# Adding two coefficient tables on GpSimd before the token products of the last three chunks of a one-core vision tower

## The chip, the cores and the metric

The kernel runs on one core of one Trainium2 chip. The metric is the device time of one execution, in microseconds (us), as the median of several executions. Engines are named PE (TensorE), DVE (VectorE), ACT (ScalarE), POOL (GpSimd) and SP (the queue that issues most DMAs).

## The reference, cut to what matters

The input `x` has shape (16, 256, 64, 2): 16 images, 256 channels h, 64 complex coefficients n. A first layer turns it into tokens; attention, an MLP and a tree of gates follow. Only the first layer is touched:

```python
dtA = A * dt[:, None]
dA = (1.0 + dtA / 2) / (1.0 - dtA / 2)
C_term = C * B[None]                                  # C is x, as complex numbers
V = jnp.exp(jnp.log(dA)[:, :, None] * jnp.arange(L))  # powers 0 to 255 of dA
K = 2.0 * jnp.einsum('chn,hnl->chl', C_term, V).real  # (16 images, 256 channels, 256 positions)
```

## The kernel before, in words

All data are float32. The exponent l of a power is split in three: a shift d (ND = 4 of them), an a (NA = 8) and an e (NE = 8), so that 4 x 8 x 8 = 256. For a channel, the result is a product over 128 rows, which are the real and the imaginary parts of the 64 coefficients: `Wa` and `Wb` (tiles of [128, 2, CH, B, ND], two buffers, by the chunk's parity) hold the image's coefficients turned by the 4 shifts, 16 images x 4 shifts = 64 columns for a channel, and `M` ([128, 2, CH, NA, NE]) holds the 64 powers of (a, e). `Wa` takes the coefficients times the real part of the shift, `Wb` the crosswise coefficients times the imaginary part; both are multiplied by the same `M` and added in PSUM. Column d = 0 of `Wb` is set to zero once, at the start; column d = 0 of `Wa` is the coefficients themselves.

The 256 channels go in 16 chunks of CH = 16. For a chunk n:

- SP loads its coefficients `craw` (`load_c`, L364), which waits for POOL's count `wdone` of the chunk two before it.
- POOL makes `Wa` and `Wb` for d = 1 to 3 (`rotate`, L510, the operation is at L522, 128x768), and waits for the token products two chunks before (`tokmm`), whose buffer it reuses.
- ACT fills d = 0 of `Wa` and e = 0 of `M` (`operands`, L702), and copies the X and Y tables to PSUM (`tables`, L709).
- DVE makes two products (`single_product`, L1178, the operation is at L1150, 128x896), into PSUM (`Ma[0]`) and into SBUF (`Mb`), and adds them into `M` for e = 1 to 7 (`single_sums`, L1185, L1190).
- PE makes the token products (`tokens`, L1641, the matmuls at L1652): 16 channels x 2 products; even channels write PSUM rows 0 to 63, odd ones rows 64 to 127. The profile shows two matmul instructions for each product. Then ACT copies the bank to `tokev` (`token_row`, L715, L719), and SP stores it (`store_h0`, L383).

Chunk 10 (`SINGLE`) is made in another way, in `unsummed_products` (DVE, L1170) and `unsummed_tokens` (PE, L1656): DVE writes its two products to `M` and `Mc` and doesn't add them, and PE makes four products per channel, `Wa` and `Wb` each with `M` (64 columns) and with `Mc` (56 columns, into the places e = 1 to 7, L1672).

From chunk FIRST = 12 on, the chunks are interleaved with the first steps of the next stage: step s = n - 12 goes with chunk n. A step takes two images of a half of the channels through norm 1, q, k and v:

- DVE: `norm1_stats(s + 3)` (L1223, L1226), then POOL: `scales` (L525: L530, L531, L533), then DVE: `norm1_apply` (`xh`, L1234), two steps ahead of its use.
- PE: `y_transposes(s + 1)` (L1688, needs `xh` of that step), `q_products(s)` (L1692), `kv_products(s, 0)` and `(s, 1)` (L1703, whose matmuls stand at L343 to L345), then the tokens of chunk n, in this order.
- ACT: `token_row(n - 1)`, `y_high(s + 1)` (L756, L761 and L764), `q_parts(s)`, `operands(n + 1)`, `tables(n + 1)`, `kv_parts` (L774).
- DVE: the products and the sum of chunk n, `y_low(s + 1)` (L1251), `q_elu(s)` (L1260), `norm1_apply(s + 2)`, `norm1_stats(s + 3)`, `k_elu` (L1271).
- POOL, for n = 12, 13, 14: `rotate` of chunk n + 1, then `scales(n - 9)`; then `scales(6)` and the later ones.

The order on each engine is the order in which the program writes it, and every wait is written by hand. Steps 4 and later have no chunk. Steps run to 15, and from then on a loop over groups of 512 tokens does the attention, the MLP and the tree.

Of the kernel before, what the change touches and what calls it, by code (L numbers as in the profile page):

```python
# [5 lines left out]
ALU = mybir.AluOpType  # L6
# [13 lines left out]
NE = 8  # L20
NA = 8
ND = 4
SH = NA * NE
CH = 16
# [16 lines left out]
STEPS = 2 * GROUPS  # L41
FIRST = 12
SINGLE = 10
SPREAD = STEPS - 5
STATS = {4: (7,), 5: (8,), 6: (9,), 7: (10, 11), 8: (12,), 9: (13,), 10: (14,), 11: (15,)}
LEVELS = 8
# [16 lines left out]
def vit_tower(nc, logdt, inv_ar, a_im, b_ri, c_ri, n1g, n1b, qkvT, projT, proj_b, n2g, n2b, fc1T, fc1_b,  # L63
              fc2T, fc2_b, wq, routersT, leafT, woutT, wout_b, consts, out):
    with ExitStack() as ctx:
# [248 lines left out]

        def added(n):

            return n + 1 - (n >= SINGLE)

        def sums_before(c):
            return max([x for x in range(c) if sums_bank(x) == sums_bank(c)], default=-1)  # L320
# [28 lines left out]
        def _(sp):  # L349
# [14 lines left out]
            def load_c(it, par):  # L364

                n = 2 * it + par
                sp.wait_ge(c0done, CREDIT + n - 1)
                sp.wait_ge(wdone, CREDIT + 2 * n - 3)
                sp.dma_start(craw[:, par, 0, :, :], c_ri[:, :, bass.ds(n * CH, CH), :].rearrange(
                    "r n h c -> (r n) h c")).then_inc(cld[par], 16)  # L370
                sp.wait_ge(wdone, CREDIT + 2 * (n - 1))
                for r in range(2):
                    sp.dma_start(craw[r * N:(r + 1) * N, par, 1, :, :],
                                 c_ri[1 - r, :, bass.ds(n * CH, CH), :]).then_inc(crossld[par], 16)
# [102 lines left out]
        def _(pool):  # L477
# [32 lines left out]
            def rotate(it, par):  # L510
# [3 lines left out]
                for x, w in enumerate((Wa, Wb)):  # L514
                    if x == 0:
                        pool.wait_ge(cld[par], CREDIT + 16 * (it + 1))
                    else:
# [4 lines left out]
                    pool.tensor_tensor(w[:, par, :, :, 1:ND].rearrange("p h c d -> p d h c"), c, u,  # L522
                                       ALU.mult).then_inc(wdone, 1)

            def scales(s):  # L525

                pool.wait_ge(st1, CREDIT + 4 * (s + 1))
                v = mv1[:, s, :, 1]
                pst = pst1[:, s, :, :]
                pool.tensor_scalar(pst[:, 0, :], v, EPS, None, ALU.add).then_inc(r1done, 1)  # L530
                pool.tensor_scalar(pst[:, 1, :], v, 1.0 + EPS, EPS * EPS, ALU.mult, ALU.add).then_inc(r1done, 1)  # L531
                pool.wait_ge(r1done, CREDIT + 3 * s + 2)
                pool.tensor_tensor(mr[:, 1:3, s // GROUPS, image(s, 0):image(s, 0) + 2], pst[:, 0:2, :],  # L533
                                   halfpow[:, :, 0:2], ALU.pow).then_inc(r1done, 1)
# [15 lines left out]
            scales(2)  # L550
            pool.wait_ge(xh1, CREDIT + 2 * 2 + 2)
            for n in range(FIRST, CHUNKS - 1):
                rotate((n + 1) // 2, (n + 1) % 2)
                scales(n - FIRST + 3)
            scales(CHUNKS - FIRST + 2)
            pool.wait_ge(b1copied, 1)
# [498 lines left out]
        def _(dve):  # L1055
# [114 lines left out]
            def unsummed_products(n):  # L1170
# [4 lines left out]
                product(n, 7, 0, M[:, n % 2, :, :, 1:NE])  # L1175
                product(n, 7, 1, Mc[:, :, :, :])

            def single_product(n, r):  # L1178

                if r == 0:  # L1180
                    dve.wait_ge(xyld, CREDIT + n + 1)
                    dve.wait_ge(vdone, CREDIT + added(n - 1))
                product(n, 7, r, (Ma[0], Mb[:, :, :, :])[r])
# [109 lines left out]
            norm1_stats(2)  # L1293
            for n in range(FIRST, CHUNKS):
                s = n - FIRST
                if s > 0:
                    single_product(n, 0)
                    single_product(n, 1)
                single_sums(n)
                if s == 0:  # L1300
                    norm1_apply(1)
                    norm1_apply(2)
                if s > 0:
                    y_low(s + 1)
                q_elu(s)
                if s > 0:
                    norm1_apply(s + 2)
                else:
                    k_elu(s, 0)
                    y_low(s + 1)  # L1310
                norm1_stats(s + 3)
                if s > 0:
                    k_elu(s, 0)
                k_elu(s, 1)
# [325 lines left out]
        def _(pe):  # L1640
            def tokens(n, par, b):  # L1641
# [11 lines left out]
                                       M[:, par, i, :, :].rearrange("p a e -> p (a e)"), start=x == 0, stop=x == 1)  # L1653
                mm.then_inc(tokmm, 1)

            def unsummed_tokens(n):  # L1656

                pe.wait_ge(wdone, CREDIT + 2 * (n + 1))
# [109 lines left out]
            for n in range(FIRST, CHUNKS):  # L1768
# [6 lines left out]
                    y_transposes(s + 1)  # L1775
                kv_products(s, 1)
                pe.wait_ge(tokout, CREDIT + n)
                tokens(n, n % 2, None)

            def step(s):  # L1780
                if s + 1 < STEPS:
# [309 lines left out]
```

## Time and profile before

| | |
|---|---|
| median of 3 runs | 489.0 us (487.67 to 489.45) |
| the profiled execution | 489.43 us, its span 487.6 us |
| PE busy | 439.4 us (90% of the span) |
| DVE, ACT, POOL busy | 346.5, 295.8, 192.2 us |
| token products at L1652 | 960 matmul instructions, 39.7 to 107.8 us |
| chunks 12 to 15 with steps 0 to 3 | about 80 to 108 us |

The span runs from the first to the last instruction; the execution's own time is 1.8 us longer. Chunks 13, 14 and 15 are the PE stretches at L1652 that begin at 92.2, 99.0 and 105.9 us. Busy time of PE is modelled at its end: consecutive matmuls overlap, so the distance between starts is what one costs.

### The profile page before, as it was taken

How to read it: one execution, taken by the hardware profiler on the slowest of the kernel's cores; microseconds unless marked ns; L12 is line 12 of the kernel's file. 1: busy time of each engine (PE TensorE's matmuls, PEld its weight loads, DVE VectorE, ACT ScalarE, POOL GpSimd, SP SyncE). 2: the span in 40 equal slices, each digit the busy share in tenths (PEclk: the TensorE clock that was granted, in tenths of full speed). 3: DMA queues.
4: the chain of work that ended last, by engine and by line, in shares of the span. 5: the costliest groups of instructions: out<-in, count | busy, mean ns of one | idle time of the engine just before them, and what ended most of it. 6: DMA issues, size and time to landing. Idle time of an engine off the chain costs nothing.

```text
span 487.6 us, 11439 instructions
## 1 busy us (share of the span) xinstructions
PE 439.4 (90%) x3881; PEld 401.9 (82%) x3881; DVE 346.5 (71%) x814; ACT 295.8 (61%) x620; POOL 192.2 (39%) x188
## 2 busy tenths in 40 slices
PE   1367778999999999999999999999999999998994
PEld 0157667887798898988998998998998998998994
DVE  5999987887876785537576576576586486484685
ACT  5754655979867686457357357357366367366552
POOL 0796997832423010516306306306306406405221
PEclk9877999999999999999999999999999999999998
DMA  4543777436343102001002002002002001001002
GB/s 130 175 149 82 177 191 219 115 88 171 98 135 102 37 33 64 3 1 44 1 2 86 0 0 86 0 0 86 0 0 86 0 0 43 0 0 44 2 1 86
DMA packets 39903, 30.95 MB, mean 63 GB/s; under 512 B 19520, under 2 KB 35264, under 8 KB 39872
## 3 DMA queue, kind: packets, MB, share of 16 engines
q1 hardware_dynamic: 28864, 27.41, 18.8%
q10 hardware_dynamic: 11008, 3.15, 2.8%
q8 instruction: 16, 0.26, 0.2%
q14 instruction: 15, 0.12, 0.1%
HBM read 17.97 MB, written 12.58 MB: 63 GB/s over the span
## 4 chain that ended last, share of the span: by engine, by line
PE 70%; DVE 9%; POOL 7%; issue 6%; ACT 4%; DMA 2%; DVEq 0%; POOLq 0%; SPq 0%; ACTq 0%
PE PS L343 20%; PE PS L345 19%; PE PS L344 19%; PE PS L1679 5%; PE PS L1721 3%; POOL Wb L522 3%; PE PS L1652 2%; DVE bst L1381 2%; PE PS L1688 1%; PE PS L1806 1%; POOL Wa L522 1%; DVE gl L1404 1%; DMA h<-h_scratch 1%; DMA iar<-in_inv_ar 1%; DVE outb L1435 1%
## 5 line engine op out<-in xcount | busy, mean ns | idle before, releaser
L877 ACT ACTIVATE PS<-PS,fc1bias 128x512 f32<-128x512 f32 x56 | 36.8, 656 | 76.5 <-PE PS L345 76.4
L343 PE MATMUL PS<-fc2h,gh 128*128 128x256 f32 x256 | 74.8, 292 | 3.7 <-DVE gl L1404 2.3
L575 POOL TENSOR_SCALAR pst<-mv 128x4 f32<-128x4 f32 x15 | 4.3, 283 | 180.0 <-DVE pst L1388 180.0
L345 PE MATMUL PS<-fc2l,gh 128*128 128x256 f32 x256 | 71.4, 279 | 0.0
L344 PE MATMUL PS<-fc2h,gl 128*128 128x256 f32 x256 | 71.3, 279 | 0.0
L1404 DVE TENSOR_TENSOR gl<-PS,gh 128x512 fp32r<-128x512 f32 x56 | 38.6, 690 | 37.9 <-ACT gh L880 35.2
L343 PEld LDWEIGHTS PS<-fc2h,gh 128*128 128x128 f32 x256 | 48.0, 188 | 9.0 <-DVE gl L1404 3.0
L343 PE MATMUL PS<-x2Th,fc1h 128*128 (+2 forms) x144 | 54.5, 378 | 0.0
L344 PE MATMUL PS<-x2Th,fc1l 128*128 (+2 forms) x144 | 53.0, 368 | 0.0
L345 PE MATMUL PS<-x2Tl,fc1h 128*128 (+2 forms) x144 | 52.9, 367 | 0.0
L344 PEld LDWEIGHTS PS<-fc2h,gl 128*128 128x128 f32 x256 | 48.2, 188 | 0.8
L345 PEld LDWEIGHTS PS<-fc2l,gh 128*128 128x128 f32 x256 | 48.0, 188 | 0.0
L1652 PE MATMUL PS<-M,Wa 128*64 128x64 f32 x480 | 32.1, 234 | 8.3 <-ACT Wa L727 3.5
L1652 PEld LDWEIGHTS PS<-M,Wa 128*64 128x64 f32 x480 | 29.8, 144 | 11.0 <-issue 6.1
L880 ACT ACTIVATE gh<-PS 128x512 fp32r<-128x512 f32 x56 | 33.6, 599 | 2.8
L1652 PE MATMUL PS<-M,Wb 128*64 128x64 f32 x480 | 31.5, 230 | 0.0
L345 PEld LDWEIGHTS PS<-x2Tl,fc1h 128*128 128x128 f32 x144 | 27.1, 188 | 4.7
L1652 PEld LDWEIGHTS PS<-M,Wb 128*64 128x64 f32 x480 | 29.8, 146 | 0.0
L343 PEld LDWEIGHTS PS<-x2Th,fc1h 128*128 128x128 f32 x144 | 27.1, 188 | 2.5
L344 PEld LDWEIGHTS PS<-x2Th,fc1l 128*128 128x128 f32 x144 | 27.2, 189 | 2.3
L522 POOL TENSOR_TENSOR Wa<-craw,U 128x768 f32<-128x768 f32 x16 | 26.4, 1652 | 6.5 <-PE PS L1652 4.2
L522 POOL TENSOR_TENSOR Wb<-craw,U 128x768 f32<-128x768 f32 x16 | 26.5, 1656 | 0.0
(259 smaller groups left out, 1407.4 us busy)
## 6 DMA issues: line engine op xcount, KB each, us to landing
h<-h_scratch SPq DMA_DIRECT2D x16, 256.0 KB, 3.4
q_scratch<-qe SPq DMA_DIRECT2D x16, 256.0 KB, 2.3
qf<-q_scratch SPq DMA_DIRECT2D x16, 256.0 KB, 3.0
out_tokens<-outb SPq DMA_DIRECT2D x14, 256.0 KB, 2.3
h_scratch<-tokev ACTq DMA_DIRECT2D x10, 256.0 KB, 3.2
craw<-in_c_ri SPq DMA_DIRECT2D x16, 128.0 KB, 2.6
craw<-in_c_ri SPq DMA_DIRECT2D x32, 64.0 KB, 2.4
h_scratch<-tokev SPq DMA_DIRECT2D x6, 256.0 KB, 2.9
```

The costliest lines, as they stand in the source:

```text
L343: pe.matmul(dst, ah, bh, start=start, stop=False, **kw)
L344: pe.matmul(dst, al, bh, start=False, stop=False, **kw)
L345: return pe.matmul(dst, ah, bl, start=False, stop=stop, **kw)
L522: pool.tensor_tensor(w[:, par, :, :, 1:ND].rearrange("p h c d -> p d h c"), c, u, ALU.mult).then_inc(wdone, 1)
L877: act.activation(bank(j % 2), bank(j % 2), ACT.Gelu, bias=fc1bias[:, j:j + 1]).then_inc(gact, 1)
L880: act.activation(gh[:, j % 2, :], bank(j % 2), ACT.Copy).then_inc(gact, 1)
L1381: dve.bn_stats(bst[:, t, :], x[:, t, :]).then_inc(done, 1)
L1404: dve.tensor_tensor(gl[:, j % 2, :], bank(j % 2), gh[:, j % 2, :].bitcast(F32), ALU.subtract).then_inc(gldone, 1)
L1435: dve.tensor_tensor(outb[:, 2 * b:2 * b + 2, :], PS[:, 6 + b, :].rearrange("p (t d) -> p t d", t=2), o1[:, 2 * b:2 * b + 2, :], ALU.add).t ...
L1652: mm = pe.matmul(dst, w[:, par, i, :, :].rearrange("p c d -> p (c d)"), M[:, par, i, :, :].rearrange("p a e -> p (a e)"), start=x == 0, st ...
L1679: mm = pe.transpose(PS[:, b + k, t * P:(t + 1) * P], src[:, t, k * P:(k + 1) * P], ident)
L1721: mm = pe.matmul(PS[:, sums_bank(c), k * (P + 1):(k + 1) * (P + 1)], key, value, start=half == 0 and k == 0, stop=half == 1, skip_group_ch ...
```

## The change

For chunks 13 to 15, POOL adds `Wb` onto `Wa` (d = 1 to 3) after it has made both, so that PE needs one product per channel in place of two. For chunk 15, DVE no longer adds its two products: it writes the first one to `M` and the second one to `Mb`, and PE makes a product with each. The count `wdone` now grows by three for these chunks, and the waits on it are rewritten to the same events as before (`made`). Chunk 12 and the earlier ones are as before.

```diff
+APART = 15
         def added(n):
-            return n + 1 - (n >= SINGLE)
+            return n + 1 - (n >= SINGLE) - (n >= APART)
+        def made(n):
+            return 2 * (n + 1) + max(0, n - FIRST)
...
             def load_c(it, par):
-                sp.wait_ge(wdone, CREDIT + 2 * n - 3)
+                sp.wait_ge(wdone, CREDIT + made(n - 3) + 1)
...
-                sp.wait_ge(wdone, CREDIT + 2 * (n - 1))
+                sp.wait_ge(wdone, CREDIT + made(n - 3) + 2)
...
+            def summed(n):
+                rotate(n // 2, n % 2)
+                pool.wait_ge(wdone, CREDIT + made(n - 1) + 2)
+                a, b = (w[:, n % 2, :, :, 1:ND].rearrange("p h c d -> p d h c") for w in (Wa, Wb))
+                pool.tensor_tensor(a, a, b, ALU.add).then_inc(wdone, 1)
...
             for n in range(FIRST, CHUNKS - 1):
-                rotate((n + 1) // 2, (n + 1) % 2)
+                summed(n + 1)
                 scales(n - FIRST + 3)
...
+            def apart_products(n):
+                dve.wait_ge(xyld, CREDIT + n + 1)
+                dve.wait_ge(tokmm, CREDIT + n - 1)
+                dve.wait_ge(vdone, CREDIT + added(n - 1))
+                product(n, 7, 0, M[:, n % 2, :, :, 1:NE])
+                product(n, 7, 1, Mb[:, :, :, :])
...
-                if s > 0:
+                if s > 0 and n != APART:
                     single_product(n, 0)
                     single_product(n, 1)
-                single_sums(n)
+                if n == APART:
+                    apart_products(n)
+                else:
+                    single_sums(n)
...
+            def summed_tokens(n):
+                pe.wait_ge(wdone, CREDIT + made(n))
+                pe.wait_ge(c0done, CREDIT + n + 1)
+                pe.wait_ge(m0done, CREDIT + n + 1)
+                pe.wait_ge(vdone, CREDIT + added(n))
+                for i in range(CH):
+                    rows = slice(64 * (i % 2), 64 * (i % 2) + 64)
+                    mm = pe.matmul(PS[rows, 0, (i // 2) * SH:(i // 2 + 1) * SH],
+                                   Wa[:, n % 2, i, :, :].rearrange("p c d -> p (c d)"),
+                                   M[:, n % 2, i, :, :].rearrange("p a e -> p (a e)"), start=True, stop=True)
+                mm.then_inc(tokmm, 1)
+            def apart_tokens(n):
...
+                pe.wait_ge(prodX, CREDIT + n + 1)
+                pe.wait_ge(prodY, CREDIT + n + 1)
+                for i in range(CH):
+                    rows = slice(64 * (i % 2), 64 * (i % 2) + 64)
+                    dst = PS[rows, 0, (i // 2) * SH:(i // 2 + 1) * SH]
+                    c = Wa[:, n % 2, i, :, :].rearrange("p c d -> p (c d)")
+                    pe.matmul(dst, c, M[:, n % 2, i, :, :].rearrange("p a e -> p (a e)"), start=True, stop=False,
+                              skip_group_check=True)
+                    mm = pe.matmul(dst.rearrange("p (a e) -> p a e", a=NA)[:, :, 1:NE], c, Mb[:, i, :, :], start=False,
+                                   stop=True, skip_group_check=True)
+                mm.then_inc(tokmm, 1)
...
                 pe.wait_ge(tokout, CREDIT + n)
-                tokens(n, n % 2, None)
+                if n == FIRST:
+                    tokens(n, n % 2, None)
+                elif n == APART:
+                    apart_tokens(n)
+                else:
+                    summed_tokens(n)
```

## Rows read from the trace of the kernel before

**Rows 1.** The page: busy time by engine, and the chain that ended last.

```profile
PE 439.4 (90%) x3881; PEld 401.9 (82%) x3881; DVE 346.5 (71%) x814; ACT 295.8 (61%) x620; POOL 192.2 (39%) x188
...
PE 70%; DVE 9%; POOL 7%; issue 6%; ACT 4%; DMA 2%; DVEq 0%; POOLq 0%; SPq 0%; ACTq 0%
```

**Rows 2.** The chain of waits, 86 to 125 us: start, us on the chain, what.

```profile
92.27 2.06 PE PS L1652 x64
...
112.52 0.24 PE PS L345
...
113.07 0.38 ACT PS L780
```

**Rows 3.** The timeline of PE: start, us, engine, line, what, count, idle time before.

```profile
92.20 0.34 PE L1652 MATMUL PS<-M,Wa 128*64 128x64 f32 x4
...
94.26 0.66 PE L1688 MATMUL PS<-const,xh 128*128 128x128 f32 x4
...
99.03 0.34 PE L1652 MATMUL PS<-M,Wa 128*64 128x64 f32 x4
...
100.83 0.34 PE L1652 MATMUL PS<-M,Wb 128*64 128x64 f32 x4
101.09 0.66 PE L1688 MATMUL PS<-const,xh 128*128 128x128 f32 x4
...
105.85 0.34 PE L1652 MATMUL PS<-M,Wa 128*64 128x64 f32 x4
...
107.92 0.66 PE L1688 MATMUL PS<-const,xh 128*128 128x128 f32 x4
```

**Rows 4.** The timeline of DVE in the same steps.

```profile
88.48 1.09 DVE L1150 TENSOR_TENSOR PS<-PS,Er 128x896 f32<-128x896 f32 x1
...
92.90 0.73 DVE L1234 TENSOR_SCALAR xh<-h,mv,mr 128x256 f32<-128x256 f32 x2
...
97.34 1.09 DVE L1190 TENSOR_TENSOR M<-PS,Mb 128x896 f32<-128x896 f32 x1
...
99.54 0.73 DVE L1234 TENSOR_SCALAR xh<-h,mv,mr 128x256 f32<-128x256 f32 x2
...
102.77 1.08 DVE L1150 TENSOR_TENSOR Mb<-PS,Ei 128x896 f32<-128x896 f32 x1
103.99 1.09 DVE L1190 TENSOR_TENSOR M<-PS,Mb 128x896 f32<-128x896 f32 x1
105.00 0.68 DVE L1251 TENSOR_TENSOR yl<-PS,yh 128x512 fp32r<-128x512 f32 x1
...
106.19 0.73 DVE L1234 TENSOR_SCALAR xh<-h,mv,mr 128x256 f32<-128x256 f32 x2
...
110.51 0.69 DVE L1251 TENSOR_TENSOR yl<-PS,yh 128x512 fp32r<-128x512 f32 x1 [2.01 <-ACT yh L764]
```

**Rows 5.** The timeline of PE for chunk 10: first and last rows of 16 channels.

```profile
70.89 0.30 PE L1670 MATMUL PS<-M,Wa 128*64 128x64 f32 x2 [0.74 <-issue]
...
75.47 0.27 PE L1672 MATMUL PS<-Mc,Wb 128*64 128x56 f32 x2
```

**Rows 6.** The timeline of POOL: the last tables before a step's scales, and the scales.

```profile
86.24 1.65 POOL L522 TENSOR_TENSOR Wb<-craw,U 128x768 f32<-128x768 f32 x1
88.35 0.22 POOL L530 TENSOR_SCALAR pst<-mv 128x2 f32<-128x2 f32 x1 [0.47 <-DVE mv L1226]
...
88.93 1.03 POOL L533 TENSOR_TENSOR mr<-pst,halfpow 128x4 f32<-128x4 f32 x1
89.93 1.61 POOL L522 TENSOR_TENSOR Wa<-craw,U 128x768 f32<-128x768 f32 x1
91.39 1.64 POOL L522 TENSOR_TENSOR Wb<-craw,U 128x768 f32<-128x768 f32 x1
```

**Rows 7.** Groups by line: two-input operations of POOL in other sizes, xcount | busy us, mean ns.

```profile
L597 POOL TENSOR_TENSOR o<-h,woutbias 128x1024 f32<-128x1024 f32 x7 | 16.9, 2416 | 0.0
...
L495 POOL TENSOR_TENSOR Ei<-Ei,tE 128x384 f32<-128x384 f32 x2 | 2.1, 1040 | 0.2
```

**Rows 8.** The timeline of ACT: the last piece of a step's v, and the next chunk's copy.

```profile
99.99 0.41 ACT L786 ACTIVATE vt<-PS 128x256 f32<-128x256 f32 x1
101.26 0.60 ACT L719 ACTIVATE tokev<-PS 128x512 f32<-128x512 f32 x1 [0.86 <-PE PS L1652]
```

More of the change, by code:

```diff
@@ L1654, in tokens @@
                 mm.then_inc(tokmm, 1)
+            def summed_tokens(n):
[10 more added lines that the diff above has]
+            def apart_tokens(n):
+                pe.wait_ge(wdone, CREDIT + made(n))
+                pe.wait_ge(c0done, CREDIT + n + 1)
+                pe.wait_ge(m0done, CREDIT + n + 1)
+                pe.wait_ge(prodX, CREDIT + n + 1)
[9 more added lines that the diff above has]
+                mm.then_inc(tokmm, 1)
             def unsummed_tokens(n):
```

## The prediction

> **What bounds the kernel now.** I read the page first: PE is busy for 90% of the span and holds 70% of the chain that ended last [rows 1]. Those are averages over stages, so I then read the chain of waits in the stretch that the change touches. From 92.3 us, where chunk 13's token products begin, to 112.8 us it runs on PE alone, and goes over to ACT only after step 4's products [rows 2]. So in this stretch PE's time is the kernel's time, as long as nothing else is close behind. What is close behind can't be seen in the chain; it is seen in the timelines of the other engines, held against PE's. DVE's rows for chunks 13 to 15 follow each other without an idle time in brackets, as the one at 110.51 has, and the same operation comes back every 6.64 us (`xh` at 92.90, 99.54 and 106.19 [rows 4]) against 6.83 us on PE (tokens at 92.20, 99.03 and 105.85 [rows 3]). DVE is thus nearly as full as PE, ahead of it by a few tenths of a microsecond. That is the reading on which this prediction rests.
>
> **The change part by part.**
>
> Token products of chunks 13 and 14. A block now takes 2.06 us from its first start to the start of the transposes behind it (99.03 to 101.09 [rows 3]). It holds 16 groups of four instructions; the first starts at 99.03 and the last at 100.83, so a group costs 1.80 / 15 = 0.12 us. Behind the last group lie 101.09 - 100.83 - 0.12 = 0.14 us before the transposes, once per block, which I leave as they are. Half of the groups go: 8 x 0.12 = 0.96 us, and a block then takes 1.10 us. The Trainium skill says of such an end ("TensorEngine Tiling (Array Packing)", Key Properties) that changing the tiling mode drains TensorE; by that the 0.14 us stay, and without it half of the block, 1.03 us, would go; the trace shows the 0.14 us but not their cause. The trace has no block of one product per channel. Its cost is bounded below by the 0.96 us saved, and above by nothing saved: a group of 0.12 us is two products whose even and odd channels run side by side on the two halves of PSUM rows, and if one product per channel broke that, the 16 left would take twice as long each. I take 0.96, since the four instructions that alternate do so already with two channels at a time.
>
> What is saved there is not all gained, for PE then waits for DVE:
> - Chunk 13: tokens start at 92.20, end the block at 93.30 in place of 94.26. The transposes behind it need `xh`, which DVE has at 92.90 + 0.73 = 93.63 [rows 4]; with 0.06 us for the signal they start at 93.70. Gain so far 94.26 - 93.70 = 0.56 us.
> - Chunk 14: tokens would start at 99.03 - 0.56 = 98.47, and need DVE's sum, 97.34 + 1.09 = 98.43, so 98.49. They end at 99.59; `xh` is there at 99.54 + 0.73 = 100.27, so the transposes start at 100.33 in place of 101.09. Gain so far 0.76 us. Of 1.92 us saved, PE waits for the other 1.16.
>
> Chunk 15. DVE leaves out the sum at 103.99 (1.09 us): `yl` can start at 103.86 and not at 105.00, 1.14 us earlier [rows 4]. This costs DVE nothing elsewhere: the first product goes to SBUF where it went to PSUM, and the rows for either are 1.09 (to PSUM) and 1.08 us (to `Mb`). The wait for `tokmm` that comes with it asks for chunk 13's tokens, over by then for 8 us. Before the change DVE's `xh` of step 5 (106.19) would also have been too late for a PE that is 0.8 us ahead; now it is not. PE makes two products per channel as before, the second with 56 columns for 64. Bounds: in chunk 12's form a group is 0.12 us, and narrower columns could take off up to 6%, 1.95 us for the block; in chunk 10, which has the same two forms in a row, 128 instructions take 75.47 - 70.89 = 4.58 us [rows 5], or 0.143 us per four, and 16 groups are 2.29 us, 2.43 with the fixed 0.14. I take 2.02, near the first end, since the order of channels and the number of instructions per channel are those of chunks 11 to 14; chunk 10 has eight per channel. The block starts at 105.09, well after the product at 102.77 + 1.08, and the transposes at 107.92 move to 107.11. Gain 0.8 us; by the other end 0.4.
>
> POOL. Three additions of 128x768. The nearest row is its own 128x768 product, 1.65 us, which starts the next 1.5 us later; the size below is 1.04 us for 384 elements, in place like the new one, the size above 2.42 us for 1024 [rows 6, 7]. I take 1.65 with the wait. Behind it in POOL's queue stand the scales (three instructions, 88.35 to 89.96), for which DVE's `xh` waits, and the next chunk's tables. First step: tables done at 87.89, add to 89.6, scales to 91.25, needed at 92.90. Second: tables 91.25 to 94.3, add to 96.0, scales to 97.6, needed at 99.54. Third: tables to 100.7, add to 102.35, scales to 104.0, needed at 106.19 - 1.14 = 105.05. The adds themselves are needed by the tokens at 92.20, 98.49 and 105.09. So POOL's additions are hidden, by 1.0 us at the tightest; without that cover each would cost up to 1.65. SP's queue has no instruction more and its loads wait for the same events.
>
> ACT. It copies chunk 14's tokens after an idle 0.86 us [rows 8] and ends its v at 100.40. With a gain of 0.56 us it is done at 99.84, just after the tokens (99.6), so it is nearly full too, but not late: `y_high` waits for the transposes.
>
> After chunk 15. DVE's `yl` of step 5 waits 2.01 us for ACT [rows 4], and ACT for PE; the chain stays on PE up to 112.76 and then enters ACT, which was waiting for PE [rows 2]. I find no DMA in between that would come at a fixed time, so the 0.8 us are handed on to the end.
>
> **The sum.** Profiled execution: 489.43 - 0.8 = 488.6 us, span 486.8. That execution stands 0.4 us above the median of 489.0; the median after would be 488.2 us. A difference of 0.5%, about 2.45 us, is what can be told from no change here.
>
> **The rivals.**
> 1. All of the saving is kept. DVE's rows would have to be early enough, which they would be only if its order gave way; it doesn't. For it: 1.92 us on an engine that the chain never leaves. It gives 489.0 - 2.0 = 487.0 us. 0.10.
> 2. PE saves nothing: one product per channel doesn't run two channels side by side, or chunk 15 costs as in chunk 10. With both, 489.0 + 0.4 = 489.4 us; with the second alone 488.6. 0.17 for 488.8 to 489.4.
> 3. Slower: POOL's scales come too late. The three additions add up in one queue: with a price of p each, the third scales are done at 87.9 (first tables) + 3p + 3 x 1.65 (scales) + 2 x 3.05 (tables) = 99.0 + 3p, and DVE's `xh` must then start by 107.15 or PE's transposes come after 107.92. So it decides from p = 2.7 us on. At 3.2 us, `xh` starts at 108.6, the transposes follow 0.79 us later, 1.5 us after 107.92, and the time is 490.4 us. Against it: 1024 elements take 2.42 us. 0.06.
> 4. Slower: DVE is held up while POOL adds. If it stood still for each add of 1.65 us, `xh` of the third step would come 3 x 1.65 - 1.14 (the sum left out) = 3.81 us later, done at 110.7, and the transposes at 110.8 for 107.92: some 3.0 us longer with a little more to wait for, 492.0 us. Against it: DVE's product at 88.48 runs in part beside the scales and the tables and takes 1.09 us, as the one at 102.77, with POOL near idle, takes 1.08 [rows 4, 6]. 0.03. The Trainium skill names such a case ("GPSIMD Engine Reference", Specifications: the SBUF interfaces are shared, with contention for DVE instructions with two SBUF inputs or in a two-port mode); in the rows above only `xh` reads SBUF alone, one tensor and scalars, so by the first half of that rule nothing is to be expected; no row tells the mode.
>
> **How the numbers follow.** The forecast (gain 0.4 to 1.1 us) has 0.60, the rivals 0.36, and 0.04 is left for what I don't see. The three runs of before lie 1.8 us apart, so a median can be off by half a microsecond. Only rival 4 and scatter reach beyond 0.5% upwards (over 491.4), and only rival 1 with scatter downwards (under 486.55): 0.06 faster, 0.90 within, 0.04 slower. The range goes from rival 1 to a little above rival 2, 487.0 to 489.7 us.
>
> **What would show it.** Right: a token block for chunks 13 and 14 of about 1.1 us from first start to last group's end, then PE idle for 0.4 and 0.7 us until DVE's `xh`; transposes about 93.7, 100.3 and 107.1 us; no idle time at 105.1; chunk 15's block about 2.0 us; POOL's adds near 1.6 us, with the wait for DVE's `mv` shorter or gone; `yl` of step 4 about 1.1 us earlier. Wrong: blocks that keep 1.8 us (rival 2), DVE idle before `xh` until POOL (rival 3), DVE rows longer than 1.09 us while POOL adds (rival 4), or an idle time after 112 us that takes the 0.8 us back. The forecast as a whole is wrong if the median falls by more than 2 us or rises at all.

## The result, and the profile after

The change made the kernel slower: 494.03 us (493.36 to 495.72, four runs) against 489.23 us (487.67 to 490.16, four runs) for the kernel before on the same chip, a ratio of 1.0107 [1.007, 1.0143]. The prediction was 488.2 us. The profiled execution took 493.36 us, its span 491.6 us. One later execution of the kernel before (617.57 us, mean clock 0.68) and one of the version last_only (512.49 us, 0.84) fell in a slower state of the chip, and no ratio below contains them.

The page of the kernel after, busy time by engine, as in [rows 1]:

```profile
PE 442.0 (90%) x3817; PEld 403.1 (82%) x3817; DVE 349.4 (71%) x813; ACT 295.7 (60%) x620; POOL 201.8 (41%) x191
```

Two things are odd beside [rows 1]. PE has 64 instructions fewer and is busy 2.6 us longer. POOL has three more and is busy 9.6 us longer, so an addition costs 3.2 us and not 1.65. The first of them isn't the change's doing. The windows of PE over the first 40 us, ahead of all that was changed, before and after (length, busy time, granted clock, DMA share, GB/s):

```profile
0.00:40.00 40.00, 14.35 (x62) 0.85 0.47 148
```

```profile
0.00:40.00 40.00, 17.19 (x57) 0.81 0.46 144
```

There alone PE is busy 2.84 us longer, at a lower clock, with fewer instructions. From the transposes of step 2 to those of step 5 it is busy 20.46 us before and 20.13 us after.

The timeline of PE after, chunks 13 to 15, for [rows 3]:

```profile
92.73 1.15 PE L1687 MATMUL PS<-M,Wa 128*64 128x64 f32 x32
96.66 0.99 PE L1741 MATMUL PS<-const,xh 128*128 128x128 f32 x4 [2.78 <-DVE xh L1254]
...
97.87 0.41 PE L350 MATMUL PS<-yl,qkvh 128*128 128x256 f32 x1
98.09 0.41 PE L348 MATMUL PS<-yh,qkvh 128*128 128x256 f32 x1
...
102.95 1.15 PE L1687 MATMUL PS<-M,Wa 128*64 128x64 f32 x32
104.75 0.66 PE L1741 MATMUL PS<-const,xh 128*128 128x128 f32 x4 [0.65 <-DVE xh L1254]
```

The token blocks are as predicted, 1.15 us each. But PE then stands idle for 2.78 us until DVE's `xh`, where 0.4 us was forecast. The timeline of DVE in the same steps, for [rows 4]:

```profile
93.45 3.15 DVE L1254 TENSOR_SCALAR xh<-h,mv,mr 128x256 f32<-128x256 f32 x2
96.52 0.73 DVE L1243 BATCH_NORM_STATS2 bst<-h 128x6 f32<-128x256 f32 x2
...
99.09 1.08 DVE L1162 TENSOR_TENSOR Mb<-PS,Ei 128x896 f32<-128x896 f32 x1
...
102.51 2.19 DVE L1254 TENSOR_SCALAR xh<-h,mv,mr 128x256 f32<-128x256 f32 x2
```

and that of POOL, for [rows 6]:

```profile
88.52 3.16 POOL L535 TENSOR_TENSOR Wa<-Wa,Wb 128x768 f32<-128x768 f32 x1
...
93.33 1.57 POOL L527 TENSOR_TENSOR Wa<-craw,U 128x768 f32<-128x768 f32 x1
94.78 1.67 POOL L527 TENSOR_TENSOR Wb<-craw,U 128x768 f32<-128x768 f32 x1
96.53 3.13 POOL L535 TENSOR_TENSOR Wa<-Wa,Wb 128x768 f32<-128x768 f32 x1
...
102.78 1.77 POOL L527 TENSOR_TENSOR Wb<-craw,U 128x768 f32<-128x768 f32 x1
```

This is where the time went. The pair of `xh` instructions took 0.73 us before and takes 3.15 and 2.19 us now. It began at 93.45, a tenth after POOL's `Wa`, and ended at 93.45 + 3.15 = 96.60, a tenth and a half after POOL's `Wb` (94.78 + 1.67 = 96.45). At 102.51 it again met both tables. DVE's product at 99.09 (input in PSUM) and its statistics at 96.52 (one SBUF input, small output) ran beside POOL's addition or just after it at their old durations; only `xh` was stretched. So the two engines don't merely share: an `xh` stands until the POOL instruction beside it is over. POOL's own rows grow by 0.13 us at most (`Wb` at 102.78).

The windows of the stretch after: stretch, length, busy time of PE (instructions), granted clock, DMA share, GB/s:

```profile
94.00:96.00 2.00, 0.00 (x0) 1.00 0.72 221
96.00:98.00 2.00, 1.34 (x7) 0.71 0.98 255
98.00:100.00 2.00, 2.00 (x11) 0.50 0.26 90
```

After the idle 2.78 us the granted clock fell to 0.50, the 1.2 GHz level. The products at 97.87 and 98.09 stand 0.22 us apart; at full clock, in the kernel before, it is 0.12 us. From 96.66 us until the clock is back this costs PE 1.5 us (3.70 us up to the product at 100.36, where the next step takes 2.16 to the same product). The two shorter blocks take 2 x 0.91 = 1.8 us off its busy time, so with half as many products in them PE is busy only 0.3 us less in the stretch.

### The profile page after: what moved, and what is told of

It is laid out like the page before. It is cut to its first block, busy times and chain, and to the rows that moved or that the text cites. A ratio compares the mean times of both kernels' runs of the same rounds, so it can differ in the third digit from the quotient of the medians.

```text
span 491.6 us, 11313 instructions
## 1 busy us (share of the span) xinstructions
PE 442.0 (90%) x3817; PEld 403.1 (82%) x3817; DVE 349.4 (71%) x813; ACT 295.7 (60%) x620; POOL 201.8 (41%) x191
## 3 DMA queue, kind: packets, MB, share of 16 engines
q10 hardware_dynamic: 11008, 3.15, 2.8%
## 4 chain that ended last, share of the span: by engine, by line
PE 69%; DVE 13%; issue 6%; POOL 5%; ACT 4%; DMA 1%; SPq 1%; DVEq 0%; POOLq 0%; ACTq 0%
PE PS L348 19%; PE PS L350 18%; PE PS L349 18%; PE PS L1732 5%; PE PS L1774 3%; POOL Wb L527 2%; DVE bst L1404 2%; PE PS L1675 2%; DVE xh L1254 1%; DMA qkvraw<-in_qkvT 1%; PE PS L1741 1%; PE PS L1864 1%; DVE gl L1427 1%; POOL Wa L527 1%; PE PS L1792 1%
## 5 line engine op out<-in xcount | busy, mean ns | idle before, releaser
L1675 PE MATMUL PS<-M,Wa 128*64 128x64 f32 x384 | 25.9, 235 | 8.0 <-ACT Wa L739 4.4
L1675 PEld LDWEIGHTS PS<-M,Wa 128*64 128x64 f32 x384 | 24.1, 145 | 9.6 <-ACT Wa L739 4.9
L348 PE MATMUL PS<-qkvh,yh 128*128 128x512 f32 x64 | 26.5, 414 | 0.0
L581 POOL TENSOR_TENSOR x<-x,pbias 128x1024 f32<-128x1024 f32 x8 | 19.2, 2402 | 16.7 <-ACT x L899 16.7
```

The lines of the kernel that those rows point to most:

```text
L348: pe.matmul(dst, ah, bh, start=start, stop=False, **kw)
L581: pool.tensor_tensor(x1[:, :, :], x1[:, :, :], rows(pbias), ALU.add).then_inc(x1b, 1)
L1675: mm = pe.matmul(dst, w[:, par, i, :, :].rearrange("p c d -> p (c d)"), M[:, par, i, :, :].rearrange("p a e -> p (a e)"), start=x == 0, st ...
```

## The experiments

Two theories stood at the start. **Hold**: `xh` can't finish beside a POOL instruction, and the additions move POOL's tables onto it. **Queue**: the additions make POOL's queue too long, and `xh` waits for its scales. A third question was whether PE's shorter blocks bring what was forecast. All ratios are to the kernel before, measured beside it on the same chip. Apart from the slow one, executions of the kernel before scatter from 486.94 to 490.72 us, and its medians from 488.85 to 489.42 us. So I also read where PE's transposes of step 5 start behind those of step 2, a distance of 107.92 - 87.46 = 20.46 us before.

| kernel | median, us | ratio [95%] | step 2 to step 5, us | against before |
|---|---|---|---|---|
| after (profiled above) | 494.03 | 1.0107 [1.007, 1.0143] | 23.56 | +3.10 |
| adds_alone | 492.46 | 1.0073 [1.0045, 1.0102] | 23.76 | +3.30 |
| no_adds | 488.86 | 0.9995 [0.9978, 1.0013] | 19.67 | -0.79 |
| no_pace | 491.62 | 1.0054 [1.0035, 1.0073] | | |
| after_again | 493.99 | 1.0096 [1.0065, 1.0127] | 25.10 | +4.64 |
| after_doubled | 493.05 | 1.0095 [1.0071, 1.0119] | 23.64 | +3.18 |
| after_natural | 494.07 | 1.0111 [1.009, 1.0133] | 24.85 | +4.39 |
| last_only | 487.35 | 0.9975 [0.9958, 0.9993] | 19.51 | -0.95 |
| after_paced | 493.23 | 1.0104 [1.0073, 1.0135] | 24.38 | +3.92 |
| natural_paced | 490.34 | 1.003 [1.0011, 1.0048] | 21.93 | +1.47 |
| last_unpaced | 489.84 | 1.0027 [1.0012, 1.0042] | 21.10 | +0.64 |
| last_apart | 488.99 | 1.0008 [0.9993, 1.0024] | 20.44 | -0.02 |

The kernel before had a median of 489.42 us beside adds_alone, no_adds and no_pace, 488.85 us beside the four from after_again to last_only, and 488.86 us beside the last four. no_pace has no value in the last columns because its change lies ahead of step 2.

**adds_alone: POOL adds, PE and DVE work as before.** Against after:

```diff
-            return n + 1 - (n >= SINGLE) - (n >= APART)
+            return n + 1 - (n >= SINGLE)
...
-                if n == APART:
-                    apart_products(n)
-                else:
-                    single_sums(n)
+                single_sums(n)
...
+                pe.wait_ge(wdone, CREDIT + made(n))
+                tokens(n, n % 2, None)
```

PE makes both products although `Wb` is already in `Wa`, so `Wb`'s part counts twice.

> GpSimd makes the three additions, but TensorE keeps two products per channel and VectorE its sum in all chunks, so that the second table counts twice in chunks 13 to 15. It carries the cost side of the change alone. Port theory (VectorE's xh, L1254 of the changed kernel, can't finish while a table product of GpSimd runs, and the additions of 3.14 us push the next tables onto it): the two xh pairs take about 3.15 and 2.2 us again in place of 0.73, TensorE idles some 1.8 us before the transposes of step 3 instead of 2.8 because its token block is 0.9 us longer, and the time is 493.5 to 495.5 us. Queue theory (the additions are only long, and the scales behind them come late): xh pairs of 0.73 us that start late. Theory that the cost lies in TensorE's halved products (a gap, and its clock with it): no loss here, 489 to 490 us.

The additions alone bring the loss: 1.0073, and +3.30 us in the stretch. The median, 492.46 us, is a little under the range expected; the pairs of `xh` and the idle time of PE before step 3 (1.82 us) are as expected, and the granted clock stays 1.00. Its DVE rows:

```profile
93.49 3.20 DVE L1254 TENSOR_SCALAR xh<-h,mv,mr 128x256 f32<-128x256 f32 x2
102.59 2.25 DVE L1254 TENSOR_SCALAR xh<-h,mv,mr 128x256 f32<-128x256 f32 x2
```

**no_adds: PE and DVE as after, POOL as before.** Against after:

```diff
-            return 2 * (n + 1) + max(0, n - FIRST)
+            return 2 * (n + 1)
...
-                pool.wait_ge(wdone, CREDIT + made(n - 1) + 2)
-                a, b = (w[:, n % 2, :, :, 1:ND].rearrange("p h c d -> p d h c") for w in (Wa, Wb))
-                pool.tensor_tensor(a, a, b, ALU.add).then_inc(wdone, 1)
```

The terms with `Wb` are left out of chunks 13 to 15.

> TensorE and VectorE as in the changed kernel, but GpSimd makes no additions, so that the second table is left out of chunks 13 to 15. It carries the saving side alone. Port theory and queue theory: xh pairs stay at 0.73 us, the transposes of steps 3, 4 and 5 start 0.56, 0.76 and 0.8 us earlier than before, and the time is 0.8 us under that of the kernel before, some 488.4 us. Theory that the cost lies in TensorE's halved products: 492 us or more, with a lower granted clock after the first short block.

Its PE rows:

```profile
91.92 1.15 PE L1684 MATMUL PS<-M,Wa 128*64 128x64 f32 x32
93.40 0.66 PE L1738 MATMUL PS<-const,xh 128*128 128x128 f32 x4 [0.32 <-DVE xh L1251]
...
100.04 0.66 PE L1738 MATMUL PS<-const,xh 128*128 128x128 f32 x4 [0.59 <-DVE xh L1251]
...
106.85 0.66 PE L1738 MATMUL PS<-const,xh 128*128 128x128 f32 x4
```

Its step 2 is 0.28 us earlier than before's. Moved by that, the transposes stand at 93.68, 100.32 and 107.13 us; the prediction had 93.70, 100.33 and 107.11. All that the prediction says of PE and DVE is right to 0.02 us. In the median the 0.8 us can't be seen.

**no_pace: the kernel before, without two waits of POOL for `xh`.** The kernel before holds POOL back behind `xh` at two places ahead of the stretch: its trace has an idle POOL there, "[1.04 <-DVE xh L1234]", ahead of the tables at 77.17 and 84.75 us. The prediction doesn't mention them. Against before:

```diff
-            pool.wait_ge(xh1, CREDIT + 2)
             rotate(FIRST // 2, 0)
...
             scales(2)
-            pool.wait_ge(xh1, CREDIT + 2 * 2 + 2)
```

> The kernel before, without the two waits of GpSimd for VectorE's xh ahead of the tables of chunks 12 and 13 (nothing else moved, all results the same). Port theory: the tables then run beside the first xh pairs, which take 1.5 to 3 us in place of 0.73, and the time rises by 0.5 to 3 us. Queue theory: xh pairs stay at 0.73 us, and the time stays within 0.3 us or falls.

With nothing added, the kernel becomes slower, 1.0054, and its `xh` rows show the hold. Both of these pairs took 0.74 us before:

```profile
76.33 3.13 DVE L1232 TENSOR_SCALAR xh<-h,mv,mr 128x256 f32<-128x256 f32 x2 [0.82 <-issue]
...
85.72 3.23 DVE L1232 TENSOR_SCALAR xh<-h,mv,mr 128x256 f32<-128x256 f32 x2 [0.16 <-issue]
```

PE waited for the first of them, and its clock fell behind that:

```profile
79.52 1.02 PE L1686 MATMUL PS<-const,xh 128*128 128x128 f32 x4 [3.65 <-DVE xh L1232]
```

The granted clock was 0.50 from 80 to 82 us, and the step took 86.64 - 79.52 = 7.12 us where it takes 6.11 before, so about 1.0 us of this loss is the clock's. The hold is thus not the change's own: the kernel before was open to it already, and its two waits kept clear of it.

**bench: the kernel before, and behind its end a list of instructions by themselves.** Its time is no measure of anything; its rows are. Some of what is added:

```diff
+            one(pool.tensor_tensor(strided, c, u, ALU.mult))
+            one(pool.tensor_tensor(strided, c, u, ALU.add))
+            one(pool.tensor_tensor(strided, strided, turned(1024, 1), ALU.add))
...
+                    if i in (0, 7, 8, 9):
+                        ins = dve.tensor_scalar(o, x, mv1[:, 0, 0, 0:1] if False else ones[:, 0:1], ones[:, 1:2], ALU.subtract, ALU.mult)
...
+                    elif i == 5:
+                        ins = dve.tensor_scalar(o, PS[:, 0, 0:256], ones[:, 0:1], ones[:, 1:2], ALU.subtract, ALU.mult)
```

> The kernel before, with a list of operations behind its end on GpSimd, alone, and then ten times one GpSimd operation beside three VectorE ones, all on data that is thrown away; its time is no measure. Why the addition takes 3.14 us where a table product of the same size takes 1.65: if the strided reads do it, the addition with contiguous inputs and strided output takes about 1.65, one strided input about 2.4, both 3.1, in place or not; if the operation or the in-place form does it, the addition on the product's inputs takes 3.1 as well, or the one that isn't in place 1.65. 
The timeline of POOL alone, in its order: the product's form (both inputs broadcast), an addition of that form, both inputs with a step of 16 bytes in place, the same not in place, contiguous, only the inputs with the step, only the output with it, one input with it, and last, in place, the natural walk (d innermost, three of every four elements):

```profile
487.99 1.55 POOL L669 TENSOR_TENSOR pscr<-h 128x768 f32<-128x768 f32 x1
489.62 1.54 POOL L670 TENSOR_TENSOR pscr<-h 128x768 f32<-128x768 f32 x1
491.24 3.07 POOL L671 TENSOR_TENSOR pscr<-pscr,h 128x768 f32<-128x768 f32 x1
494.39 3.07 POOL L672 TENSOR_TENSOR pscr<-h 128x768 f32<-128x768 f32 x1
497.54 1.80 POOL L673 TENSOR_TENSOR pscr<-h 128x768 f32<-128x768 f32 x1
499.42 3.06 POOL L674 TENSOR_TENSOR pscr<-h 128x768 f32<-128x768 f32 x1
502.56 1.83 POOL L675 TENSOR_TENSOR pscr<-h 128x768 f32<-128x768 f32 x1
504.46 2.19 POOL L676 TENSOR_TENSOR pscr<-h 128x768 f32<-128x768 f32 x1
...
508.80 1.99 POOL L678 TENSOR_TENSOR pscr<-pscr,h 128x768 f32<-128x768 f32 x1
```

The addition's 3.07 us come from reading both inputs with the step. Adding in place of multiplying, working in place, and the step of the output cost nothing. The change wrote the addition in the walk of the product, (d, h, c); the order of storage would have cost 1.99 us. The Trainium skill has the effect ("GPSIMD Engine Reference", Performance pitfalls for Q7 kernels): reading with a step of more than 8 bytes costs 2.9 cycles an element in place of 1.9, half as much again. The rows here agree in kind and give more for two inputs: 3.07 against 1.80, or 70%.

The timeline of DVE beside POOL additions of 3.07 us, three instructions at a time: two pointer scalars (the form of `xh`), immediates, two tensors in SBUF, scalar_tensor_tensor, input in PSUM, and two pointer scalars with 255 elements in place of 256:

```profile
514.17 3.80 DVE L1699 TENSOR_SCALAR dscr<-h,ones 128x256 f32<-128x256 f32 x3
518.08 3.59 DVE L1701 TENSOR_SCALAR dscr<-h 128x256 f32<-128x256 f32 x3
...
525.94 3.63 DVE L1705 TENSOR_TENSOR dscr<-h 128x256 f32<-128x256 f32 x3 [0.46 <-DVE dscr L1703]
529.69 4.10 DVE L1707 SCALAR_TENSOR_TENSOR dscr<-h,ones 128x256 f32<-128x256 f32 x3
533.89 1.45 DVE L1709 TENSOR_SCALAR dscr<-PS,ones 128x256 f32<-128x256 f32 x3
537.05 3.83 DVE L1711 TENSOR_SCALAR dscr<-h,ones 128x255 f32<-128x255 f32 x3 [1.72 <-POOL pscr L684]
```

Every form in this list that reads a tensor in SBUF is held, with one input or with two, and with 255 elements too, which the expectation had as a sign against a two-port mode. The one with its input in PSUM is not: it is through while POOL is still adding. The prediction's own evidence against a hold, DVE's product beside POOL's work, has its input in PSUM as well.

The Trainium skill has the rule that the prediction weighed ("GPSIMD Engine Reference", Specifications; "Advanced Engine Details and Errata", VectorE Performance Modes): GpSimd shares SBUF interfaces with VectorE, with contention for instructions with two SBUF inputs or in a two-port mode, and two-port instructions and GpSimd's block each other. The trace agrees with the first half: the tensor_tensor with two SBUF inputs is held (3.63 us for three). The second half, which the prediction left hanging, fits `xh`, which goes from SBUF to SBUF with equal shapes and is blocked. But no row shows that `xh` runs in such a mode. Its pace gives no sign of it, for a second instruction of 256 elements starts 0.33 us behind the first, and a product of 896 elements takes 1.00 us to the next.

**after_again, after_doubled, after_natural.** The change once more; then with PE making each of its products twice in chunks 13 and 14, so that PE's idle time is shorter and nothing else differs (in `summed_tokens`):

```diff
-                for i in range(CH):
+                for i in list(range(CH)) * 2:
```

and then with the addition in the natural walk:

```diff
-                a, b = (w[:, n % 2, :, :, 1:ND].rearrange("p h c d -> p d h c") for w in (Wa, Wb))
+                a, b = (w[:, n % 2, :, :, 1:ND] for w in (Wa, Wb))
```

> The changed kernel itself once more, on the chip of the next three, so that they can be compared with it: 493 to 495 us, with TensorE's transposes of step 3 at the lower clock (0.64 us from their first start to the next product in place of 0.41).

> The changed kernel with the summed products of chunks 13 and 14 made twice into the same place (same result), so that TensorE is busy 0.93 us longer ahead of the wait for xh in steps 1 and 2 and nothing else moves. Clock theory (the halved products lengthen an idle time that xh ends anyway, and only then does the granted clock fall): the idle time before the transposes of step 3 is 1.85 us and not 2.78, the granted clock stays 1.00, the following products take 0.12 and not 0.21 us each, and the time is 1.3 us under the changed kernel's, 492.5 to 493. Without that theory: the same time as the changed kernel within 0.3 us.

> The changed kernel with the addition's walk turned: channel, image, shift in place of shift, channel, image, the same elements. From the bench: 1.99 us and not 3.07. If the cost of the change comes from the length of the addition, through the tables that it pushes onto xh: xh pair of step 1 about 1.9 us and of step 2 about 0.9 us in place of 3.15 and 2.2; transposes of step 5 some 0.5 us later than before the change in place of 3.1; no fall of the clock; time 489.5 to 490.5 us. If the mere number of additions sets it, no gain over 0.5 us from the changed kernel.

The change repeats at 493.99 us. Its PE timeline, with the windows of PE as above:

```profile
96.03 0.66 PE L1741 MATMUL PS<-const,xh 128*128 128x128 f32 x4 [2.76 <-DVE xh L1254]
104.14 0.90 PE L1741 MATMUL PS<-const,xh 128*128 128x128 f32 x4 [2.07 <-DVE xh L1254]
112.49 0.66 PE L1741 MATMUL PS<-const,xh 128*128 128x128 f32 x4
```

```profile
104.00:106.00 2.00, 1.86 (x10) 0.60 0.92 245
106.00:108.00 2.00, 2.00 (x10) 0.54 0.00 0
```

Here the clock fell one step later than in the first profile and than expected, after the idle 2.07 us and not after the 2.76 us. PE was then the bound again, so it cost 112.49 - 104.14 = 8.35 us where the step takes 6.83 before, 1.5 us. With the products doubled, the idle times are 1.88 and 1.15 us and the clock stays at 1.00:

```profile
95.64 0.66 PE L1741 MATMUL PS<-const,xh 128*128 128x128 f32 x4 [1.88 <-DVE xh L1254]
103.77 0.66 PE L1741 MATMUL PS<-const,xh 128*128 128x128 f32 x4 [1.15 <-DVE xh L1254]
```

Doubling PE's work in two blocks did not slow the kernel (493.05 against 493.99 us, ratios that overlap). The gain of 1.3 us that was expected of it isn't shown either. So PE's saving is worth nothing here, and can cost: what is saved becomes idle time, and after that the clock may fall. The natural walk made each addition 1.99 us and the kernel no faster (494.07 us, where 489.5 to 490.5 was expected). `xh` was held for 1.39 and 2.25 us, the second time by the tables' end and by the addition itself, and the clock fell behind the idle 2.84 us:

```profile
93.09 2.12 DVE L1254 TENSOR_SCALAR xh<-h,mv,mr 128x256 f32<-128x256 f32 x2
101.11 2.98 DVE L1254 TENSOR_SCALAR xh<-h,mv,mr 128x256 f32<-128x256 f32 x2
```

**The sum from these rows.** DVE had 0.76 us to spare at step 4 (`xh` of [rows 4] done at 99.54 + 0.73, 0.06 for the signal, transposes at 101.09). If the hold is the cause, the transposes of step 4 are late by the two stretches less that 0.76 us. Before, they stand 101.09 - 87.46 = 13.63 us behind those of step 2.

| kernel | `xh` longer than 0.73 by | less 0.76 | measured, step 2 to step 4 less 13.63 |
|---|---|---|---|
| after | 2.42 + 1.46 | 3.12 | 3.12 |
| adds_alone | 2.47 + 1.52 | 3.23 | 3.21 |
| after_again | 2.43 + 1.47 | 3.14 | 3.12 |
| after_doubled | 2.48 + 1.49 | 3.21 | 3.19 |
| after_natural | 1.39 + 2.25 | 2.88 | 2.85 |
| last_unpaced | 1.59 | 0.83 | 0.83 |

The hold accounts for all of it to 0.03 us, and PE's saving enters nowhere. In the step behind it PE is the bound again, and only the clock adds more than 0.1 us (1.5 us in after_again and after_natural).

**after_paced, natural_paced: hold POOL's tables back behind `xh`, as the kernel before does earlier.** This takes the hold away and leaves the queue. Against after and after_natural:

```diff
             for n in range(FIRST, CHUNKS - 1):
+                if n > FIRST:
+                    pool.wait_ge(xh1, CREDIT + 2 * (n - FIRST + 2) + 2)
                 summed(n + 1)
```

> The changed kernel, with GpSimd waiting for VectorE's xh of steps 3 and 4 before it makes the tables of chunks 14 and 15, so that no table product runs beside an xh; the addition is the slow one, 3.14 us. Theory that the hold is all of the loss: xh pairs of 0.73 us, and the time back near 488.5 us. Theory that GpSimd's queue alone (3.05 tables + 3.15 addition + 1.65 scales = 7.85 us per step, against 6.65 to 6.83 on the other engines) is a bound of its own: xh pairs of 0.73 us, but late ones; transposes of step 4 at 102.5 and of step 5 at 111.3 us on the time scale of before (101.09 and 107.92), 3.4 us later, time 492.4 us, and 1.5 more if the clock falls.

> The same pace with the faster addition of 1.99 us. Per step GpSimd then needs 6.75 us. Worked through in the same way: xh pairs of 0.73 us; transposes of step 4 at 101.35 and of step 5 at 108.95 us on the time scale of before, 1.0 us later; idle times of TensorE under 1.5 us, so no fall of the clock; time 490.0 us, 4 us under the same kernel without the pace (494.1).

All pairs of `xh` are back at 0.73 or 0.74 us, but those of steps 4 and 5 are late. For natural_paced, POOL's next table, which waits for `xh`, and DVE's `xh`, which waits for POOL's scales:

```profile
101.58 1.60 POOL L527 TENSOR_TENSOR Wa<-craw,U 128x768 f32<-128x768 f32 x1 [1.03 <-DVE xh L1256]
```

```profile
100.64 0.73 DVE L1256 TENSOR_SCALAR xh<-h,mv,mr 128x256 f32<-128x256 f32 x2 [1.13 <-issue]
```

The profile names no engine for this last wait, but POOL's scales end at 99.52 + 1.03 = 100.55 us, just ahead of it. Now `xh`, tables and scales form a ring: a step of POOL is its tables (3.1 us), its addition (2.1), its scales (1.6) and the wait for `xh` (1.0), together 7.86 us from one `Wa` to the next (93.72 to 101.58), where PE needs 6.83. In after_paced, with 3.2 us for the addition, it is 9.06 us for two steps running. The clock fell there too (0.76 from 99 to 106 us), but PE still waited for `xh` before each of the transposes, so the ring set the pace. Three additions thus fit in neither order: unpaced they are paid for by the hold, paced by the queue.

**last_only, last_unpaced, last_apart: one addition, for chunk 15 alone, in the natural walk.** POOL makes no table behind chunk 15's and has room there. last_only against before:

```diff
                 rotate((n + 1) // 2, (n + 1) % 2)
+                if n + 1 == CHUNKS - 1:
+                    pool.wait_ge(xh1, CREDIT + 2 * 4 + 2)
+                    pool.wait_ge(wdone, CREDIT + 2 * CHUNKS)
+                    a, b = (w[:, 1, :, :, 1:ND] for w in (Wa, Wb))
+                    pool.tensor_tensor(a, a, b, ALU.add).then_inc(wdone, 1)
                 scales(n - FIRST + 3)
...
-                tokens(n, n % 2, None)
+                if n == CHUNKS - 1:
+                    summed_tokens(n)
+                else:
+                    tokens(n, n % 2, None)
```

last_unpaced against last_only:

```diff
-                    pool.wait_ge(xh1, CREDIT + 2 * 4 + 2)
```

last_apart against after, with the addition in the natural walk; it keeps the change's form of chunk 15, two products on PE and no sum on DVE:

```diff
-            return 2 * (n + 1) + max(0, n - FIRST)
+            return 2 * (n + 1) + (n >= APART)
...
             def summed(n):
                 rotate(n // 2, n % 2)
+                if n < APART:
+                    return
+                pool.wait_ge(xh1, CREDIT + 2 * 4 + 2)
...
-                if n == FIRST:
+                if n < APART:
                     tokens(n, n % 2, None)
```

> The kernel before, with the addition for chunk 15 alone, walked as in the faster form, and behind a wait for VectorE's xh of step 4, when GpSimd was idle for 1.0 us anyway; TensorE makes one product per channel there, VectorE still adds its two. If cost and saving are understood: addition 2.0 us from about 100.3, no xh pair over 0.75 us, transposes of step 5 at 106.97 in place of 107.92 (0.93 us earlier, by then DVE's xh is just there), time 0.9 us under that of before, 488.3 to 488.7 us.

> The kernel with the one addition for chunk 15, without its wait for xh of step 4: the addition then starts at 99.4 and xh at 99.54 us of the time scale of before. If an addition in this place holds xh as the table products do: xh pair of step 4 about 2.25 us in place of 0.73, transposes of step 4 at 101.9 and of step 5 at 108.5 us, 1.5 us later than with the wait, time 489.5 us. If only table products hold it: as with the wait, 487.4 to 488 us, or a little less.

> The third part of the change without its trouble: one addition for chunk 15, the faster form, behind the wait for xh of step 4; VectorE leaves its sum out and TensorE makes a product with each of its two products, as in the changed kernel. TensorE is the bound there, so this gives VectorE 1.1 us that nobody waits for and costs TensorE the 0.9 us that the addition saved: block of chunk 15 of 2.0 us, transposes of step 5 at 107.85 us on the time scale of before (107.92), no gain, 489 us and 0.9 us over the kernel in which VectorE sums.

last_only is the version that beats both kernels: 487.35 us, 0.9975 [0.9958, 0.9993]. The stretch explains 0.95 us of it; that the median lies 1.5 us lower, below the range expected, is within its interval. Its rows:

```profile
99.97 2.00 POOL L558 TENSOR_TENSOR Wa<-Wa,Wb 128x768 f32<-128x768 f32 x1 [1.04 <-DVE xh L1239]
```

```profile
105.47 1.15 PE L1669 MATMUL PS<-M,Wa 128*64 128x64 f32 x32
106.59 0.66 PE L1706 MATMUL PS<-const,xh 128*128 128x128 f32 x4
```

Chunk 15's block takes 106.59 - 105.47 = 1.12 us for 2.06, and the transposes follow without a wait. Without the wait for `xh` the same addition starts at 98.63, over `xh` at 98.78, which then takes 2.32 us, and the gain of 0.95 us becomes a loss of 0.64 us (1.0027). With the form apart it is -0.02 us: PE pays for its second product what DVE no longer pays for the sum, and DVE was not the bound there. In the transposes both are as expected, to 0.1 us.

## Why the prediction was wrong

**Wrong: "So POOL's additions are hidden, by 1.0 us at the tightest."** This is the step that failed, in both of its halves.
- The price. I took 1.65 us from POOL's product of the same size. The addition measures 3.13 to 3.16 us. The product's inputs are broadcast; the addition's are read with a 16-byte step. The rows of 384 and 1024 elements, which I took as bounds, are of other walks too. A row of the same engine, operation and size was no bound, since its walk was another.
- What it stands beside. I counted the time until the scales are needed, and did not ask what POOL would be doing while `xh` runs. In [rows 4, 6] chunk 14's second table ends at 91.39 + 1.64 = 93.03 us and `xh` begins at 92.90, so the two hardly meet. Anything put ahead on POOL moves the tables over `xh`. With additions of 1.65 us they would have lain from 91.25 to 94.3 us, over it too; after_natural, with 1.99 us, shows what that costs. So the right price alone would not have saved the forecast.

**Rival 4 had the kind right and the object wrong.** It let DVE stand for the whole of each addition, 4.95 us in all, and gave 492.0 us. In the profiled run after, it was the tables, not the additions, that held DVE, and only at `xh`: 3.88 us in two pairs. An addition holds `xh` as well where it meets it, as in after_natural and last_unpaced. I gave the rival 0.03 because DVE's product at 88.48 is not slowed "beside the scales and the tables". That row ends at 89.57, before the tables begin at 89.93 [rows 4, 6]. The next one did run beside them at the old pace:

```profile
89.48 1.08 DVE L1150 TENSOR_TENSOR Mb<-PS,Ei 128x896 f32<-128x896 f32 x1
```

But neither bears on `xh`, whose input is in SBUF.

**Rival 3** (scales too late, from 2.7 us on) was sized by the queue alone. At 3.2 us it gave 490.4 us. But in the change itself `xh` started when it should have in step 3 (93.45 less the 0.54 us by which this run was late is 92.91, for 92.90 before). The queue's part was to bring tables and `xh` together.

**Rivals 1 and 2** are out: PE's blocks were 1.15 us, and nothing of the saving was kept.

**Right:** the groups of 0.12 us, the fixed 0.14 us of a block, the waits that PE's saving turns into, DVE's missing sum, chunk 15's block at about 2.0 us, all of it by no_adds, to 0.02 us in each of the transposes. "Of 1.92 us saved, PE waits for the other 1.16" says that the time is DVE's once PE is faster, and that is why a held `xh` was so dear.

**Not in the sum: the clock.** Every term was taken at full clock. Idle times of 2.07 to 3.65 us were followed by the lower level in four profiles (after, after_again, after_natural, no_pace), and not in one case (2.76 us in after_again, step 3). Idle times of 1.88 us and less before the transposes were not, except in after_paced, where 1.76 us before the tokens and 1.31 us before the transposes have only the tokens between them. Where PE was the bound next, it cost 1.5 us.

**What stays open.** The profiled run is 3.93 us longer than that of before: 3.10 in the stretch, 0.54 ahead of it and 0.29 behind it. The 0.54 us are within the scatter of step 2's start (86.70 to 88.06 us over the profiles other than no_pace's) and belong to no part of the change that I found. The medians differ by 4.8 us; how much of the rest is the clock in executions without a profile was not measured. The queue without the hold could be tried only with pacing, which adds its own wait.

## What to carry to other kernels

Before work is moved to GpSimd, write down for each VectorE instruction that reads SBUF what GpSimd does at that time, after the move: here every one with all its tensors in SBUF, but for the statistics, ended only after the GpSimd tensor_tensor that it met, so that 0.41 us became 1.7 (`xh` in after) or 3.2 (bench). A wait of GpSimd for such an instruction can be what keeps them apart (`xh1` here), and one wait more turned a loss of 0.6 us into a gain of 0.95. Price a GpSimd operation by a row with the same walk of its inputs, not the same size, and put it where its queue has nothing that others wait for.

## What the runs showed of the hardware

- VectorE's tensor_scalar, tensor_tensor and scalar_tensor_tensor from SBUF to SBUF don't finish beside a GpSimd tensor_tensor (128x256 float32 here). It isn't a slowdown in proportion: a pair met by two GpSimd instructions ends 0.14 to 0.15 us after the second. GpSimd loses 0.16 us at most (the bench's first addition, 3.23 us); but in all meetings except that one a GpSimd instruction was already running when VectorE's began, and what a longer VectorE instruction that begins first would do to it isn't shown. An input in PSUM, and statistics of one SBUF tensor, run at their old pace.
- GpSimd's tensor_tensor of 128x768 float32 takes from 1.54 us (broadcast inputs) to 3.07 us (both inputs with a step of 16 bytes), by the walk of its inputs alone.
- Work taken off TensorE ahead of a wait can come back as a lower clock: behind an idle 2.78 us the granted clock fell to 0.50 and 128x256 products came 0.22 us apart for 0.12. Of the 1.8 us of busy time that two shorter blocks saved, the clock took 1.5 back. With the same products made twice the idle time was 1.88 us and the clock stayed at 1.00; but it stayed there after one idle 2.76 us as well.
